# Unread products between the turned tiles of two feed-forwards and of the latent attention, taken out

## What is computed

```python
x = x + tanh(g_xattn[0]) * _L0_xattn_ref(_layernorm(x), ctx, ...)   # softmax(QK)·ctx
x = x + tanh(g_ffn[0])   * _L0_ffn_ref(_layernorm(x), ...)          # base matmul + top-2 of 8 rank-16 experts
x = x + tanh(g_xattn[1]) * _L1_xattn_ref(_layernorm(x), ctx, ...)   # windowed attention over 16 positions
x = x + tanh(g_ffn[1])   * _L1_ffn_ref(_layernorm(x), ...)          # base matmul + routed rank-16 experts
x = x + tanh(g_xattn[2]) * _L2_xattn_ref(_layernorm(x), ctx, ...)   # latent attention, 16 heads of 32
x = x + tanh(g_ffn[2])   * _L2_ffn_ref(_layernorm(x), ...)          # products with the signs of a weight
x = x + tanh(g_xattn[3]) * _L3_xattn_ref(_layernorm(x), ctx, ...)   # 32 heads of 128
x = x + tanh(g_ffn[3])   * _L3_ffn_ref(_layernorm(x), ...)          # top-2 of 4 rank-16 experts
```

## Time and profile before

| | |
|---|---|
| median of 3 runs | 2014.16 us (2009.43 to 2020.78) |
| the profiled execution | 2009.42 us |
| its span in the profile | 2007.7 us |
| TensorE's granted clock, mean over the span | 0.969 of full |
| TensorE matmuls busy | 1828.4 us, 91% |
| VectorE busy | 1604.0 us, 80% |
| GpSimd busy | 717.6 us, 36% |
| ScalarE busy | 589.1 us, 29% |

### The profile page before, as it was taken

One profiled execution on the slowest core, in us unless ns is written; L12 is line 12 of the kernel. 1 busy time (PEld: TensorE's weight loads), 2 busy tenths in 40 slices (PEclk: granted clock), 3 DMA queues, 4 the chain that ended last, 5 costly groups with the idle time before them and its releaser, 6 DMA issues. The chain is left out here.

```text
span 2007.7 us, 37794 instructions
## 1 busy us (share of the span) xinstructions
PE 1828.4 (91%) x14970; PEld 1040.8 (52%) x15120; DVE 1604.0 (80%) x2908; ACT 589.1 (29%) x1371; POOL 717.6 (36%) x810
## 2 busy tenths in 40 slices
PE   8779989999899898998947999999999999999986
PEld 6434565446654466454624555555555555555543
DVE  4678775987679876798738888888888888888895
ACT  2422242223432233322324222222222222222353
POOL 3530242302432114411125434444443434343552
PEclk9889999999999998999978999999999999999998
DMA  8658204472045601464045111021111111111011
GB/s 252 188 160 236 80 10 148 117 199 74 10 153 161 198 26 37 142 180 121 7 128 164 54 48 52 24 74 32 54 53 48 47 50 53 54 33 33 12 43 53
DMA packets 146493, 180.97 MB, mean 90 GB/s; under 512 B 47248, under 2 KB 84784, under 8 KB 146320
## 3 DMA queue, kind: packets, MB, share of 16 engines
q1 hardware_dynamic: 144304, 177.33, 30.2%
q10 hardware_dynamic: 2016, 1.22, 0.3%
HBM read 134.86 MB, written 43.66 MB: 89 GB/s over the span
## 5 line engine op out<-in xcount | busy, mean ns | idle before, releaser
L1426 POOL TENSOR_TENSOR early_vare<-early_mv,w_eps 128x1 f32<-128x1 f32 x96 | 30.9, 322 | 540.5 <-DVE early_mv L1537 531.1
L2450 POOL TENSOR_TENSOR la_q<-la_straight,la_rot 128x512 f32<-128x512 f32 x128 | 163.3, 1275 | 159.4 <-DVE la_rot L2544 159.4
L443 PE MATMUL la_ps<-w_xTl,w_wqh 128*128 128x512 bf16 x512 | 196.1, 383 | 23.5 <-issue 18.3
L444 PE MATMUL la_ps<-w_xTh,w_wql 128*128 128x512 bf16 x511 | 195.4, 382 | 0.0
L443 PE MATMUL la_ps<-w_wol,la_oTh 128*128 128x512 bf16 x512 | 194.0, 379 | 0.3
L444 PE MATMUL la_ps<-w_woh,la_oTl 128*128 128x512 bf16 x512 | 194.0, 379 | 0.0
L442 PE MATMUL la_ps<-w_woh,la_oTh 128*128 128x512 bf16 x506 | 191.8, 379 | 0.9 <-DVE la_oTl L2572 0.9
L2463 POOL TENSOR_TENSOR la_p<-la_s,la_rec 128x256 f32<-128x256 f32 x128 | 90.3, 705 | 272.4 <-DVE la_rec L2565 272.4
L2350 ACT ACTIVATE la_oTh<-la_ps 128x256 bf16<-128x256 f32 x256 | 84.2, 381 | 292.9 <-PE la_ps L2229 292.9
L442 PE MATMUL la_ps<-w_xTh,w_wqh 128*128 128x512 bf16 x389 | 149.6, 385 | 7.5 <-DVE la_rot L2544 3.9
L1703 DVE TENSOR_TENSOR early_products<-early_pR,early_vR 128x4096 f32<-128x4096 f32 x32 | 140.1, 4420 | 18.1 <-DMA early_pR<-scr_p 13.2
(11 more groups left out here) (354 smaller groups left out, 4663.5 us busy)
## 6 DMA issues: line engine op xcount, KB each, us to landing
early_vR<-scr_v SPq DMA_DIRECT2D x128, 257.0 KB, 5.7
early_wkv<-wkv SPq DMA_DIRECT2D x32, 512.0 KB, 4.5
la_v<-v SPq DMA_DIRECT2D x64, 256.0 KB, 3.8
k<-early_ctxt SPq DMA_DIRECT2D x32, 256.0 KB, 3.9
v<-early_ctxt SPq DMA_DIRECT2D x64, 128.0 KB, 2.8
scr_p<-early_weights SPq DMA_DIRECT2D x16, 512.0 KB, 5.2
early_pR<-scr_p SPq DMA_DIRECT2D x32, 256.0 KB, 3.9
w_raw_q<-in_Wq SPq DMA_DIRECT2D x8, 1024.0 KB, 7.5
```

The costliest lines, as they stand in the source:

```text
L443: pe.matmul(out, lh[c], rl[c], start=False, stop=False)
L444: ins = pe.matmul(out, ll[c], rh[c], start=False, stop=(last and c == n - 1))
L2450: rope_sum.send(pool.tensor_tensor(dst, straight[:, slot, :], rot[:, slot, :], ALU.add))
```

## The change

It takes out the three groups of four unread products at each of the sites A, B and C: 4 x 3 x 3 = 36 matmuls (with as many weight loads) in a turn, 144 in all. The calls in attention 0 and in the loop of attention 2 stay.

```diff
@@ def lora_ffn(turn, f, layer)
                 for j in range(QUAD):
-                    if j >= 1:
-                        idle_products(4, turn, "turn", layer, j)
                     turn_tile(turn, layer, j)
@@ def attention2(turn)
                 for j in range(QUAD):
-                    if j >= 1:
-                        idle_products(4, turn, "turn", 4, j)
                     turn_tile(turn, 4, j)
```

## The result

The changed kernel takes 2027.38 us (median of 14 runs, 2020.08 to 2033.95), the one before 2013.78 us beside it: a ratio of 1.0072, 95% interval [1.0061, 1.0082], so 14.5 us slower (0.0072 x 2013.8), with bounds 12.3 and 16.5; the two medians differ by 13.6. The forecast was 9.2 us and a range up to 2036.

A forecast was written before the change was run, and what follows sets the result against it. TensorE was taken to bound at A, DVE at B and C, where products keep the clock up. Terms -4.5 + 0.9 - 0.4 + 8.0 + 5.2 = +9.2 us on the 2014.2 median gave 2023.4, given as 2023; range 2011 to 2036.

The forecast's parts named there:

- Site A, -4.5 and +0.9: Turning of layer 1: 1.5 us gained in each of turns 2 to 4; first turn loses 0.9 us; no clock fall expected.
- tile 0 can start when its low half is there (332.1): Layer 1 routing: without unread products tile 0's route products start at 332.1, part of the 1.5 us gain a turn.
- Site B, +8.0: Turning of layer 3: half clock over the route and base products behind it costs 2.0 us, four times.
- what would show it wrong: Clock stays 1.00 at layers 3 and 4, route products' end moves under 1 us, or two stretches in a row.
- Site C, +5.2: Turning of layer 4, before the down-projections: shorter half-clock fall, partly in the wait, 1.3 us a turn, bounds 0 and 3.4.
- C's freed 0.1 us and the queues: Layer 4's last transposes start 0.1 us earlier, four times, -0.4; nothing in the SP, ACT, DVE and POOL queues is touched.
- The mean clock: Sign of being right: mean granted clock drops by about 0.007, to 0.96, from eight stretches of 3.4 us.
- Absorbed: Rival: lower clock at layers 3 and 4 lands in waits for DVE; +1.6 us, 2016, no change; chance 0.20.
- A falls as well: Rival: the clock also falls behind layer 1's turning, 5.1 us more than forecast, +14.3, 2028.5; chance 0.10.
- A worth its full length: Rival: all 2.6 us come through at layer 1 in four turns, other falls cost little; -10.8, 2003; chance 0.07.
- Double falls: Rival: 3.4 us lost at layers 3 and 4 each turn, 1.7 at the first layer 1; +24, 2038; chance 0.13.
- The forecast case: Whole kernel: +9.2 us, bounds +3 to +16 (2017 to 2030), chance 0.50, about half each side of 10.1.

The follow-up runs named there:

- B out: Only layer 3's turning loses its unread products, against the kernel before; 1.0056 [1.0034, 1.0079], 11.3 us slower.
- transposes: Kernel before with eight fp32 identity transposes replacing each group of four products in the turnings of layers 3 and 4; 1.0007 [0.9991, 1.0023].
- C out: Only layer 4's turning loses its unread products, against the kernel before; 1.0056 [1.0035, 1.0077], 11.3 us slower.
- A out: Only layer 1's turning loses its unread products, against the kernel before; 0.9982 [0.9967, 0.9997], in a second series 0.9980 [0.9967, 0.9992].

## Why the prediction was right, step by step

- **Site A, -4.5 and +0.9.** Right in kind: the last `xn` and the low halves are late next, and the clock stays up. The size is 1.05 to 1.22 us a turn, not 1.5. The step that was off is "tile 0 can start when its low half is there (332.1)", 2.93 us behind the first transposes: it starts 3.12 behind them (334.29 - 331.17), some 0.15 us after that low half ends, and the routing then takes as long as before (3.05 us to the same base product). So "tile 3 ends about 334.9" was too early by 0.2 us. That ACT's high halves start where they do because of a copy that waits for a DMA, the prediction took from the rows without saying so; that copy ends last here. As a whole A is worth 3.6 to 4.0 us, where I summed 3.6, with the +0.9 of the first turn in it. That term was not told apart: profiles with A's products in place (B out, transposes) also have a stretch at half clock near 86 us. That the sum came out so close is in part luck.
- **Site B, +8.0.** The price was right: 8.7 us by the change's own timeline (with the slowed last transposes of layer 4 in it), 11.3 [6.8, 15.9] alone. The picture behind it was not quite: 2.0 was taken "nearer to layer 5's rows", which have one stretch of 3.4 us, and in every turn two followed each other, which the prediction listed, for each site, under what would show it wrong (at C one turn of four had more than one). The part of the 6.8 us that lies in the wait costs little, so a turn pays 2.0 to 2.45 us of the 3.4 that they could cost. The comparison of shares was uneven too: 0.25 at B is mostly from the time that transposes hold the engine, the 0.84 of 3.40 at layer 5 from their records. By records TensorE was busy for 1.31 of 3.40 us before it fell, a share of 0.39, and it fell all the same.
- **Site C, +5.2.** The term with the largest error, if it is read from C out alone: 11.3 us [7.0, 15.5], 2.8 a turn and not 1.3. In the change's own profile it is 6.3, near the forecast. I argued that a part of the stretch lies in the wait. That holds in some turns (0.2 and 0.8 us), but I had taken one stretch of 3.4 us as the length, and in attention 2 it lasts up to 13.7. Which turns get a long one differs between the profiles, so the 5.3 us between forecast and result can't be given to C alone: by the change's timeline A, B and C together are 3.2 above their terms (11.5 against -4.5 - 0.4 + 8.0 + 5.2 = 8.3), and the rest is the first turn, other stretches that came and went, and noise, not told apart.
- **C's freed 0.1 us and the queues.** The first is there: from the first to the last transposes of layer 4 it was 4.92 us (4.91 in the first turn) and is 4.82 in every turn. For the queues nothing was seen that speaks against what was said.
- **The mean clock.** It fell by 0.012 and not by 0.007: the eight stretches are 47.7 us long together, where eight of 3.4 us were counted.
- **The rivals.** "Absorbed" fell with B out, "A falls as well" with A out and with the transposes. "A worth its full length" fell with A out: its last `xn` and low halves are waited for, and no more than 1.22 us a turn came back. "Double falls" had its mechanism half right (6.8 us at every B), but not its price.

The forecast case held with 14.5 us in its bounds of 3 to 16, near the upper one. I put the chance that it ends above 10.1 us at about half; it did.

## What to carry to other kernels

Ask of each filler product separately whether it stands in a wait or on the path: the same three groups of four matmuls cost 1.1 to 1.2 us a turn at A and saved 1.6 to 2.8 us at B and at C. A filler that fits inside the wait of a DVE-bound stage is free, and what it protects is the dense work behind it. Price a fall of the clock with a range for its length, not with one length: behind the same code it lasted 3.4 us in some turns and 13.7 in others. And count falls in more than one profile before you call a smaller filler enough.

## What the runs showed of the hardware

- fp32 transposes of the identity hold the granted clock at 1.00 as well as bf16 products that take the same time (eight against four, 1.0007 [0.9991, 1.0023], and 1.00 at B and C in all four turns).
- The clock can stay at 0.50 for 13.6 us with TensorE busy for 12.64 of them (C out, first turn), though the kernel before holds 1.00 through the same work (13.24 of 13.60 busy). Small matmuls alone do not explain it: at layer 5 it came back after 3.4 us of products with 32 columns.
- The clock fell without a gap over 1.4 us: at site B of the changed kernel's second turn TensorE had waited 1.39 us at a time, with transposes between, and in the third turn it had been busy for 1.31 of the 3.40 us before the fall.
